# Two graph layers on one Trainium2 core: half of the low coefficient tiles made by an adding DMA, code checks and bias sums moved, and layer 0's residual kept in its PSUM bank

## The reference, cut to what matters

```python
# layer 0
e0 = leaky(einsum('bid,bjd->bij', h * a0[:, 0], h))      # 0.2 slope; e1, e2, e3 for codes 2, 3, 4
alpha = sigmoid(where(adj == 1, e0, -max))
x = layernorm(x + einsum('bij,bjd->bid', alpha, x) + bias)
# layer 1
Hh = x @ W;  s = Hh @ a[:F];  d = Hh @ a[F:]
e = where(adj != 0, exp(-leaky_relu(s[:, :, None] + d[:, None, :])), 0)
x = layernorm(x + elu((e @ Hh) / rowsum(e)))
```

## Time and profile before

| | |
|---|---|
| Median of 3 runs | 1370.85 us (1370.57 to 1371.18) |
| Profiled execution, own time | 1369.6 us |
| Its span, first to last instruction | 1367.8 us |
| TensorE busy | 1275.9 us, 93% of the span |
| VectorE, ScalarE, GpSimd busy | 1029.2, 856.0, 842.4 us |
| Mean granted clock | 0.993 |

### The profile page before, as it was taken

The page is one execution under the profiler, slowest core; times in us unless marked ns, Lnnn a source line. Parts: engine busy times, 40 slices in busy tenths (PEclk is TensorE's granted clock), DMA queues, the critical chain, the costliest instruction groups (busy, mean ns, idle before and its releaser), DMA issues.

```text
span 1367.8 us, 27395 instructions
## 1 busy us (share of the span) xinstructions
PE 1275.9 (93%) x7874; PEld 1139.3 (83%) x7874; DVE 1029.2 (75%) x2594; ACT 856.0 (63%) x2130; POOL 842.4 (62%) x1228
## 2 busy tenths in 40 slices
PE   5799999999999999999999999999999998999986
PEld 4788888888888888888888888888888888888875
DVE  5777778787777877778777787877878777787865
ACT  4746757476575756757476575756757567574643
POOL 4746749476583855839466583865839567394732
PEclk9999999999999999999999999999999999999999
DMA  8162350614325162350624415153250623406001
GB/s 173 32 109 74 67 109 19 119 58 87 94 41 102 45 111 73 59 113 12 121 63 73 104 28 110 54 100 80 54 119 16 111 73 65 108 14 124 28 5 34
DMA packets 190352, 101.73 MB, mean 74 GB/s; under 512 B 140656, under 2 KB 173808, under 8 KB 190320
## 3 DMA queue, kind: packets, MB, share of 16 engines
q1 hardware_dynamic: 171888, 67.79, 21.2%
q0 software_dynamic: 18432, 33.56, 14.6%
HBM read 84.55 MB, written 16.78 MB: 74 GB/s over the span
## 4 chain that ended last, share of the span: by engine, by line
PE 39%; POOL 24%; DVE 20%; issue 11%; ACT 5%; DMA 0%; DVEq 0%; POOLq 0%; ACTq 0%
POOL coef_lo L369 13%; PE acc_bank L1227 11%; PE hh_bank L1206 5%; DVE coef L880 5%; PE acc_bank L1108 4%; PE acc_bank L1110 4%; PE acc_bank L1109 4%; PE lg_bank L1108 3%; PE lg_bank L1110 3%; PE lg_bank L1109 3%; POOL var_eps L377 3%; POOL rstd L380 2%; POOL rstd L390 2%; DVE stats L920 2%; DVE reluP L915 2%
## 5 line engine op out<-in xcount | busy, mean ns | idle before, releaser
L1227 PE MATMUL acc_bank<-H,coef 128*128 128x258 f32 x2048 | 469.1, 382 | 10.9 <-ACT reluP L606 9.6
L1227 PEld LDWEIGHTS acc_bank<-H,coef 128*128 128x128 f32 x2048 | 381.7, 190 | 73.7 <-issue 20.2
L369 POOL TENSOR_TENSOR coef_lo<-coef,coef_hi 128x1024 fp32r<-128x1024 f32 x128 | 305.7, 2389 | 62.2 <-ACT coef_hi L552 60.3
L1108 PE MATMUL acc_bank<-h_hi,coef_hi 128*128 128x256 f32 x1024 | 297.4, 290 | 0.0
L1110 PE MATMUL acc_bank<-h_hi,coef_lo 128*128 128x256 f32 x1024 | 286.3, 280 | 0.0
L1109 PE MATMUL acc_bank<-h_lo,coef_hi 128*128 128x256 f32 x1024 | 286.1, 279 | 0.0
L880 DVE SCALAR_TENSOR_TENSOR coef<-tr_bank,E_col,codeT 128x256 f32<-128x256 f32 x512 | 209.1, 476 | 39.3 <-PE acc_bank L1227 36.8
L1108 PEld LDWEIGHTS acc_bank<-h_hi,coef_hi 128*128 128x128 f32 x1024 | 194.8, 190 | 1.0
L1109 PEld LDWEIGHTS acc_bank<-h_lo,coef_hi 128*128 128x128 f32 x1024 | 195.0, 190 | 0.0
L1110 PEld LDWEIGHTS acc_bank<-h_hi,coef_lo 128*128 128x128 f32 x1024 | 194.7, 190 | 0.0
L552 ACT ACTIVATE coef_hi<-coef 128x1024 fp32r<-128x1024 f32 x128 | 135.7, 1060 | 84.6 <-DVE coef L819 84.1
(11 more groups left out here) (77 smaller groups left out, 2283.5 us busy)
## 6 DMA issues: line engine op xcount, KB each, us to landing
code_nat<-in_adj POOLq DMA_DIRECT2D x128, 256.0 KB, 5.3
x_raw<-in_x SPq DMA_DIRECT2D x16, 1024.0 KB, 5.6
out<-x SPq DMA_DIRECT2D x128, 128.0 KB, 1.7
codeT<-code_nat SPq DMA_TRANSPOSE x128, 3.3
W_ext<-in_L_gnn_W SPq DMA_DIRECT2D x1, 256.0 KB, 4.2
eluE<-in_L_gnn_a SPq DMA_DIRECT2D x1, 256.0 KB, 4.6
bias_bc<-in_L_gnn_bias SPq DMA_DIRECT2D x1, 128.0 KB, 4.1
a_col<-in_L_gnn_a SPq DMA_DIRECT2D x4, 1.0 KB, 4.6
```

The source lines that it names most:

```text
L369: nc.gpsimd.tensor_tensor(coef_lo[:, t % 4, :, :], blocks(coef[:, t % 4, :]), f32(coef_hi[:, t % 4, :, :]), ALU.subtract).then_inc(S.lo0, 1)
L1108: nc.tensor.matmul(dst, lhs_hi, rhs_hi, start=first, stop=False)
L1227: ins = nc.tensor.matmul(acc_bank[t % 2][:, 0:HC], coef[:, SLOT1[t], J * P:(J + 1) * P], H[:, J, :], start=J == 0, stop=J == NT - 1)
```

## The change

Five things are changed.

1. Layer 0's low parts of tiles 4 to 7. ScalarE now makes a second copy behind the high one: `coef_lo = -1.0 * coef`, rounded to fp32r as `coef_hi` is, so it is `-coef_hi`. GpSimd then issues a DMA that adds `coef` (SBUF, 512 KB) onto `coef_lo` (SBUF, 512 KB). Each of the four tiles has its own semaphore `lo0_added`. Tiles 0 to 3 are made by the subtraction on GpSimd as before.
2. On GpSimd, `low0` stands before `next_bias` in a step, not behind it.
3. On ScalarE, `watch_codes` of tile 0 stays in step 0, those of 1, 2, 3 move to steps 5, 6, 7, those of 4 and 5 stand between score chunks 3 and 4 and between chunk 4 and `keep_H(7)`, and those of 6 and 7 behind chunks 5 and 6.
4. The residual of layer 0 is written in place in `acc_bank` (PSUM); `stats0` and `norm0` read it there. `resid` is gone.
5. So TensorE may write that bank again only when `norm0` has read it: `aggregate0(t)` for t >= 2, and the first two `aggregate1`, wait for `x1` and no longer for `resid0`.

```diff
             def low0(S, b, t):
                 pool.wait_ge(S.hi0, NT * b + t + 1)
-                nc.gpsimd.tensor_tensor(coef_lo[:, t % 4, :, :], blocks(coef[:, t % 4, :]),
-                                        f32(coef_hi[:, t % 4, :, :]), ALU.subtract).then_inc(S.lo0, 1)
+                if S is F and t >= 4:
+                    pool.sem_inc(pool_past, 1)
+                    pool.dma_start(f32(coef_lo[:, t % 4, :, :]), blocks(coef[:, t % 4, :]),
+                                   accum_op=ALU.add).then_inc(F.lo0_added[t % 4], 16)
+                else:
+                    nc.gpsimd.tensor_tensor(coef_lo[:, t % 4, :, :], blocks(coef[:, t % 4, :]),
+                                            f32(coef_hi[:, t % 4, :, :]), ALU.subtract).then_inc(S.lo0, 1)
...
+                    if 1 <= t and t + 3 < NT:
+                        low0(F, b, t + 3)
                     if nxt and t >= 2:
                         if t == 2:
                             pool.wait_ge(F.x_loaded, 16 * (b + 2))
                         next_bias(b, t - 2)
-                    if 1 <= t and t + 3 < NT:
-                        low0(F, b, t + 3)
...
-                nc.scalar.activation(coef_hi[:, t % 4, :, :], blocks(coef[:, t % 4, :]),
-                                     ACT.Copy).then_inc(S.hi0, 1)
+                ins = nc.scalar.activation(coef_hi[:, t % 4, :, :], blocks(coef[:, t % 4, :]), ACT.Copy)
+                if S is F and t >= 4:
+                    ins = nc.scalar.activation(coef_lo[:, t % 4, :, :], blocks(coef[:, t % 4, :]), ACT.Copy,
+                                               scale=-1.0)
+                ins.then_inc(S.hi0, 1)
...
-                    if t < 6:
+                    if t < 1:
                         watch_codes(b, t)
...
-                    if t in (6, 7):
-                        watch_codes(b, t)
+                    if 5 <= t < 8:
+                        watch_codes(b, t - 4)
                 keep_H(F, b, 6, prev, False)
                 keep_x1T(F, b, 7, prev)
                 if nxt:
                     scale_scores(b + 1, 3)
+                watch_codes(b, 4)
                 if nxt:
                     scale_scores(b + 1, 4)
+                watch_codes(b, 5)
                 keep_H(F, b, 7, prev, False)
                 ends_H(F, b)
                 if nxt:
                     scale_scores(b + 1, 5)
+                watch_codes(b, 6)
                 if nxt:
                     scale_scores(b + 1, 6)
+                watch_codes(b, 7)
...
-                nc.vector.scalar_tensor_tensor(resid[:, t % 2, :], acc_bank[t % 2][:, 0:D], 0.5, xb[:, t, :],
+                nc.vector.scalar_tensor_tensor(acc_bank[t % 2][:, 0:D], acc_bank[t % 2][:, 0:D], 0.5, xb[:, t, :],
                                                ALU.mult, ALU.add).then_inc(S.resid0, 1)
-                nc.vector.bn_stats(stats[:, t % 2, :], resid[:, t % 2, :]).then_inc(S.stats0, 1)
+                nc.vector.bn_stats(stats[:, t % 2, :], acc_bank[t % 2][:, 0:D]).then_inc(S.stats0, 1)
-                nc.vector.tensor_scalar(x1[:, t, :], resid[:, t % 2, :], moments[:, t % 2, 0:1],
+                nc.vector.tensor_scalar(x1[:, t, :], acc_bank[t % 2][:, 0:D], moments[:, t % 2, 0:1],
                                         rstd[:, t % 2, :], ALU.subtract, ALU.mult).then_inc(S.x1, 1)
...
                 elif 2 <= t < 6:
-                    dve.wait_ge(F.lo0, NT * b + t + 4)
+                    for i in range(2):
+                        dve.wait_ge(F.lo0_added[t - 2 + i], 16 * b + 16)
...
-                pe.wait_ge(S.lo0, NT * b + t + 1)
+                if S is GEN:
+                    pe.wait_ge(GEN.lo0, NT * b + t + 1)
+                elif t < 4:
+                    pe.wait_ge(F.lo0, 4 * b + t + 1)
+                else:
+                    pe.wait_ge(F.lo0_added[t % 4], 16 * b + 16)
                 if t >= 2:
-                    pe.wait_ge(S.resid0, NT * b + t - 1)
+                    pe.wait_ge(S.x1, NT * b + t - 1)
...
                 if t >= 2:
                     pe.wait_ge(S.relu, NT * b + t - 1)
                 else:
-                    pe.wait_ge(S.resid0, NT * b + t + 7)
+                    pe.wait_ge(S.x1, NT * b + t + 7)
```

More of the change, by code:

```diff
@@ L66, in __init__ @@
         self.lo0 = sem(tag + "lo0")
+        if not general:
+            self.lo0_added = [sem(tag + f"lo0_added{i}") for i in range(4)]
         self.agg0 = sem(tag + "agg0")
@@ L194, in two_graph_layers @@
         coef_lo = sb("coef_lo", [P, 4, NT, P], FP32R)
-        resid = sb("resid", [P, 2, D])
         stats = sb("stats", [P, 4, 6])
@@ L246, in two_graph_layers @@
         sp_past = sem("sp_past")
+        pool_past = sem("pool_past")
         flag_step = sem("flag_step")
@@ L802, in mask0_below @@
                 if t >= 4:
-                    dve.wait_ge(F.lo0, NT * b + t - 3)
+                    dve.wait_ge(F.lo0, 4 * b + t - 3)
                 elif prev:
```

## The result

The changed kernel takes 1422.7 us (median of 4 runs, 1420.23 to 1425.67), the kernel before 1370.7 us in the same comparison: ratio 1.0381, 95% interval 1.0359 to 1.0403, so 52 us or 3.8% slower. I had forecast 1392 us with a range of 1381 to 1425. The direction was right, and the time lies inside the range, but the loss is two and a half times the 21 us that I had worked out. The profiled execution of the changed kernel took 1420.23 us, its span is 1418.5 us, and its graphs stand 85.9 us apart (the first matmuls of two aggregate0(2) at 480.30 and 566.22), where I had forecast 83.9 and the kernel before has 82.6.

The account below looks back on a forecast made before the run. TensorE, busy 93% of the span, was taken as the bound. Per graph +1.7 - 2.75 + 0.55 + 1.8 = +1.3 us, times sixteen 20.8, on 1369.6 plus 1.25: 1392 us; 8-in-10 range 1381 to 1425.

Parts of the forecast that it names:

- The wait of aggregate0(2): First loop, TensorE: aggregate0(2) now waits for x1(0) and starts 1.7 us later a graph, bounds 1.5 to 1.9.
- The old waits, -2.75: TensorE's waits of 1.58, 0.62, 0.55 us at the x1 transposes of tiles 1 to 3 all go: -2.75 us a graph.
- the other two go in the same way: Waits ahead of the transposes of tiles 2 and 3, 0.62 and 0.55 us, vanish as tile 1's 1.58 does.
- What is late next, +0.55: Tile 4: ScalarE's second copy keeps high_xT(3) and x1(4) no earlier, so 0.5 of the loop's 1.05 us gain stays.
- the moved bias, "inside the -0.5": GpSimd: next_bias behind a wait for ScalarE delays power0 by at most 0.7 us in steps 3 to 5, within the loop's -0.5.
- The checks at the end: Two code checks ahead of keep_H(7) on ScalarE delay TensorE's chunk 7 by 1.8 us a graph, bounds 1.4 to 2.1.
- The DMA: Adding DMA for low parts of tiles 4 to 7 takes 5.6 us, bounds 3.4 to 11.1; hidden within 7.7 us.
- the rival of the slow DMA: Adding DMA takes 11.1 us, 3.4 short in each graph: 1446 us, or 1412 us at 9 us; chance 0.13.
- PSUM for norm0 at nothing: norm0 on VectorE reading PSUM takes what it took from SBUF, 0.40 to 0.41 us; priced at nothing on the path.
- a sign of being wrong: The forecast counts as wrong if norm0 from PSUM takes more than 0.5 us.
- the loop gives nothing back: ScalarE's copies hold keep_x1T and high_xT, the old waits return: loop +1.7, graph +3.5, 1427 us; chance 0.10.
- The end is hidden: keep_H(7)'s delay does not reach TensorE, so only the loop counts: 1363 us, at best 1354; chance 0.07.

Follow-up runs that it names:

- the fastest kernel: Changed kernel with residual in SBUF, code checks where ScalarE has room, all eight next_bias behind the code loads: 1344.1 us, 0.9816 of the kernel before.

## Why the prediction was right and wrong

- **The wait of aggregate0(2)**: forecast 1.7, bounds 1.5 to 1.9; it is 1.50 in the graph shown and 22.5 us in 15 graphs. Right, at the lower bound.
- **The old waits, -2.75**: this step failed. I argued that TensorE, late by 1.7, would find x1(1) ready, which holds, and that "the other two go in the same way", which does not: tiles 2 and 3 stand at 1.87 and 1.02 and tile 4 at 0.27. x1(2) hangs on what TensorE does behind the held aggregate0(2): the transpose of x1(0), which starts the row keep_x1T(0), tile 5's high and low parts, power0(2), norm0(2). In each pair that differs in the bank alone, norm0(2) keeps its distance to keep_x1T(0) (one graph each):

| Kernel | keep_x1T(0) starts | norm0(2) starts | distance, us |
|---|---|---|---|
| before | 466.19 | 473.81 | 7.62 |
| before, residual in PSUM | 477.43 | 485.03 | 7.60 |
| changed | 483.62 | 490.89 | 7.27 |
| changed, residual in SBUF | 474.72 | 481.99 | 7.27 |
| bias behind the code loads, SBUF | 457.80 | 464.10 | 6.30 |
| bias behind the code loads, PSUM | 467.81 | 474.05 | 6.24 |

  Only a result whose making does not pass the new wait can catch up: tile 1's. In the third pair neither a bias nor a subtraction stands between the moments of tiles 2 to 4 and their norms on GpSimd, and the residual in PSUM still costs 27.7 us. Even with the bias put back, 0.84 + 0.23 + 0.26 = 1.33 us of old waits are left: -1.42, not -2.75. A small slip beside it: TensorE would have asked for x1(1) at 469.34 - 1.58 + 1.7 = 469.5, not 469.2.
- **What is late next, +0.55, and the moved bias, "inside the -0.5"**: this was the costliest step. I looked for the next late thing on ScalarE at tile 4, and treated the bias as a matter of GpSimd's load, which fell. It is a matter of its order: the end of the issue, which I had priced at nothing and which takes 0.91, and the bias of 1.03 stand in front of power0. The swap moves norm0(2) by 1.03 us, and TensorE's wait for tile 3 stands at 1.02 with it and at 0.23 without. Undone, it gives 25 us, and the loop is even with before, where I had it 0.5 shorter. What I had looked for at tile 4 is there too, and small: low_xT(3), ahead of norm0(4), waits for ScalarE,

```profile
500.21 0.69 DVE L782 TENSOR_TENSOR hT_lo<-lg_bank,hT_hi 128x512 fp32r<-128x512 f32 x1 [0.72 <-ACT gT_hi L502]
```

  and TensorE then stands 0.27 us idle for x1(4). By the graph shown the loop came out at +1.9, not -0.5: 16 x 2.4 = 38 us of error, of which the checks below gave some 8 back.
- **The checks at the end**: 1.8 forecast, 1.28 of idle in the timeline, 24 us over all graphs when undone (1.5 a graph). The mechanism is right, the size a little high: from a check's start to that of what follows go 518.82 - 517.68 = 1.14 us, where I had put 1.27, and chunk 3 to keep_H(7) takes 515.60 to 518.82 on ScalarE, 3.22 us, where it took 1.76: 1.46 later, not 1.78.
- **The DMA**: 5.6 us with bounds 3.4 to 11.1. The page of the changed kernel:

```profile
coef_lo<-coef POOLq DMA_DIRECT2D x64, 512.0 KB, 4.6
```

  It lands after 4.6 us (4.5 to 5.0), no aggregation waits for it, and the rival of the slow DMA is out. By the formula of the Trainium skill (DMA: Bandwidth & Descriptors, section "Anatomy of one DMA") I estimate about 3.2 us for a plain copy of 512 KB; no run here has such a copy on GpSimd's queue. The adding one takes 1.4 us more than that estimate, and nothing in the sum hangs on it.
- **PSUM for norm0 at nothing**: wrong in size, small in effect. Groups by form (count, busy us, mean ns): of norm0 in the kernel before with only the residual moved, and then in the fastest kernel, from SBUF:

```profile
L849 DVE TENSOR_SCALAR x<-acc_bank,moments,rstd 128x256 f32<-128x256 f32 x128 | 69.2, 541 | 54.0 <-POOL rstd L380 54.0
```

```profile
L861 DVE TENSOR_SCALAR x<-resid,moments,rstd 128x256 f32<-128x256 f32 x128 | 52.6, 411 | 63.3 <-POOL rstd L389 63.3
```

  541 against 411 ns: 0.13 us more, and over the 0.5 us that I had named as a sign of being wrong. The rule of the Trainium skill that I left out (VectorE: DVE Perf Modes, "Why PSUM operands drop a tier") gave just that, and the trace agrees. It also shows the other side: beside a busy GpSimd norm0 from SBUF took 0.80, from PSUM it stays at 0.54 to 0.55 (485.03 above).
- **The rivals**: "the loop gives nothing back" had chance 0.10 and gave 1427 us. That is the outcome in size (1423) and in its number for the loop (+1.7 against +1.9). But its cause, ScalarE's copies holding keep_x1T and high_xT, accounts for at most the 0.27 us of tile 4: with both copies in place and only the bias put back, the loop waits no more than before. "The end is hidden" is out by the checks' 24 us.
- **The range**: that 1422.7 lies inside 1381 to 1425 is luck. I had drawn its upper part for a slow DMA and for ScalarE's copies, and it was neither.

## What to carry to other kernels

A wait put ahead of an instruction is repaid only by later waits whose result does not depend on that instruction or on anything behind it in the same engine's list; follow the chain of each old wait back, through the other engines' lists too, and see on which side of the new one it passes. When a long operation on a queue is replaced by a short one that waits for more, ask what stands behind it: here 2.4 us less work brought norm0(2) only 0.35 us nearer to keep_x1T(0) (7.27 us for 7.62), and 1.38 us with the swapped call put back (6.24); that one call cost 25 us. And find the free places of an engine by its timeline before moving work to it: the same adding DMA cost 9 us with the checks where they were and gained 7 us with the checks moved, and the kernel with the queues cleared is 26 us faster than before.

## What the runs showed of the hardware

TensorE's granted clock falls for a short time after some waits. A wait in the changed kernel, and the stretches around it (start and end, length, busy time of PE, PEld, DVE, ACT and POOL, granted clock, DMA share, GB/s):

```profile
233.53 0.44 PE L1203 MATMUL xt_bank<-ident,x 128*128 128x128 f32 x2 [1.87 <-DVE x L865]
```

```profile
231.00:232.00 1.00, 0.66 (x6) 0.36 (x3) 1.00 (x2) 0.25 (x1) 1.00 (x2) 1.00 0.92 180
232.00:233.00 1.00, 0.00 (x0) 0.00 (x0) 0.54 (x3) 0.42 (x1) 0.81 (x2) 1.00 1.08 205
233.00:234.00 1.00, 0.47 (x4) 0.47 (x5) 1.00 (x3) 1.00 (x2) 0.00 (x0) 1.00 0.75 139
234.00:235.00 1.00, 1.00 (x9) 1.00 (x8) 1.00 (x4) 1.00 (x6) 0.00 (x0) 0.71 0.00 0
235.00:236.00 1.00, 1.00 (x6) 1.00 (x6) 0.81 (x3) 1.00 (x4) 0.83 (x2) 0.50 0.00 0
236.00:237.00 1.00, 1.00 (x7) 1.00 (x6) 0.99 (x1) 0.68 (x2) 1.00 (x3) 0.50 0.46 90
237.00:238.00 1.00, 1.00 (x7) 1.00 (x7) 0.99 (x2) 0.00 (x0) 0.92 (x2) 0.58 1.11 213
```

TensorE had stood idle for 1.87 us up to 233.53. It then ran at 0.50, the 1.2 GHz level, for parts of four us: over the ten us from 230 the granted clock is 0.83, 1.7 us lost. Four of the graphs have this behind the 1.87 us wait (at 230, 660, 920 and 1260), and in them TensorE, late by the clock, finds x1(3) and x1(4) ready and doesn't wait the 1.0 and 0.2 us. That is one reason why the list of waits grew by less than the time. In the others, as in the graph shown above, the same wait leaves the clock at 1.00, and I can't say from these runs what decides it. Over the span the mean granted clock is 0.993 before, 0.989 in the changed kernel and 0.984 with only the residual in PSUM. There the waits are 16.6 us longer in all and 0.9% of 1397 us is 12.6 us, which makes 29.2 of the span's 29.7. For the changed kernel the same estimate gives 40.4 + 0.4% of 1418 us, 46.1 of 50.7; the rest I can't place. In these runs some waits on TensorE cost more than their length, and I had no term for it.

In the changed kernel an operation of one column on GpSimd (var_eps) takes 0.93 us at tile 2, beside VectorE's SBUF-to-SBUF products, and 0.64 and 0.52 at tiles 0 and 1. The issue of the adding DMA takes GpSimd 0.91 us, and it stands in front of the norm.
